# Two-layer cross-attention on one core: where the next batch's layer-0 projections stand among the heads of layer 1

## What is computed

```python
q = hidden_state @ Wq + bq          # layer 0: 32 heads of 16
k = encoder_hidden_state @ Wk + bk  # 8 heads of 16
v = encoder_hidden_state @ Wv + bv
scores = einsum('bkgld,bksd->bkgls', q, k) * scale + mask
out = einsum('bkgls,bksd->bkgld', softmax(scores), v) ... @ Wo + bo
x = layer_norm(out + hidden_state) * gamma + beta

a = layer_norm(audio_kv)            # layer 1, audio_kv is the same context
Q, K, V = hidden_states @ Wq.T, a @ Wk.T, a @ Wv.T    # 16 heads of 32
out = einsum('bhts,bhsd->bhtd', softmax(Q K^T * scale), V) @ Wo.T
return hidden_states + tanh(gate) * out
```

## Time and profile before

| | us |
|---|---|
| median of 3 runs | 1476.19 |
| lowest and highest run | 1471.12, 1485.24 |
| the profiled execution | 1483.69 |
| its span, first to last instruction | 1481.9 |
| mean granted clock of TensorE in it | 0.941 |

### The profile page before, as it was taken

The page is one execution under the profiler, slowest core; times in us unless marked ns, Lnnn a source line. Parts: engine busy times, 40 slices in busy tenths (PEclk is TensorE's granted clock), DMA queues, the critical chain, the costliest instruction groups (busy, mean ns, idle before and its releaser), DMA issues.

```text
span 1481.9 us, 32160 instructions
## 1 busy us (share of the span) xinstructions
PE 1390.0 (94%) x9840; PEld 1008.5 (68%) x9840; DVE 822.4 (55%) x2470; ACT 827.6 (56%) x2504; POOL 183.5 (12%) x200
## 2 busy tenths in 40 slices
PE   3999999999999999999999999999999999999997
PEld 3667676676767667676676766767676776767765
DVE  4435656565564655646465565656646465564643
ACT  3535746476464756646475564646646475564644
POOL 2100111010011101111020111101011110111100
PEclk8559999999999999999999999999999999999996
DMA  8434254534425453344544424453443544434250
GB/s 238 151 94 92 69 122 99 136 82 119 100 70 120 110 134 70 96 111 86 128 108 109 98 71 117 99 136 77 119 100 75 120 110 121 83 81 109 51 133 6
DMA packets 77581, 153.76 MB, mean 104 GB/s; under 512 B 10272, under 2 KB 46944, under 8 KB 76784
## 3 DMA queue, kind: packets, MB, share of 16 engines
q1 hardware_dynamic: 77552, 153.40, 43.9%
HBM read 113.72 MB, written 39.65 MB: 103 GB/s over the span
## 4 chain that ended last, share of the span: by engine, by line
PE 79%; issue 6%; DVE 6%; ACT 4%; DMA 1%; POOL 1%; SPq 1%; ACTq 0%; DVEq 0%; POOLq 0%
PE TP L363 21%; PE PJ L317 12%; PE SCO L354 10%; PE OA L389 5%; PE PJ L553 4%; PE PJ L411 4%; PE PJ L419 4%; PE PJ L330 4%; PE SCO L358 3%; PE OA L394 2%; ACT PR L864 1%; PE PJ L425 1%; DVE SCO L672 1%; ACT PT L877 1%; DMA PT<-wk 1%
## 5 line engine op out<-in xcount | busy, mean ns | idle before, releaser
L864 ACT ACTIVATE PR<-SCO,MN 100x361 f32<-100x361 f32 x768 | 434.1, 566 | 362.1 <-DVE MN L672 337.4
L672 DVE CUSTOM_DVE_ANT_0 SCO<-SCO,MK 100x361 f32<-100x361 f32 x768 | 413.0, 541 | 381.1 <-PE SCO L354 259.2
L363 PE MATMUL TP<-ident,PR 100*121 100x100 f32 x2304 | 438.7, 303 | 34.3 <-ACT PT L877 28.4
L363 PEld LDWEIGHTS TP<-ident,PR 100*121 100x121 f32 x2304 | 342.6, 200 | 143.2 <-issue 89.7
L877 ACT ACTIVATE PT<-TP 121x300 f32<-121x300 f32 x576 | 239.2, 415 | 6.1 <-PE TP L363 6.0
L354 PE MATMUL SCO<-K0S,Q0S 64*100 64x362 f32 x512 | 213.8, 418 | 11.2 <-DMA K0S<-k_scr 10.1
L354 PEld LDWEIGHTS SCO<-K0S,Q0S 64*100 64x100 f32 x512 | 83.9, 164 | 128.0 <-issue 99.7
L864 ACT ACTIVATION_READ_ACCUMULATOR PR<-SCO,MN 100x1 f32 x768 | 151.5, 197 | 0.0
L358 PE MATMUL SCO<-K1S,Q1S 128*100 128x362 f32 x256 | 111.8, 438 | 3.1 <-ACT Q1S L947 1.2
L999 POOL TENSOR_TENSOR TL<-AT,TH 128x363 fp32r<-128x363 f32 x64 | 64.0, 1001 | 393.8 <-ACT TH L922 393.8
L672 DVE DVE_READ_ACCUMULATOR2_ANT MN<- 100x1 f32 x768 | 108.5, 141 | 0.0
(11 more groups left out here) (124 smaller groups left out, 1821.5 us busy)
## 6 DMA issues: line engine op xcount, KB each, us to landing
K1S<-k_scr SPq DMA_DIRECT2D x128, 364.0 KB, 6.4
k_scr<-K1HL SPq DMA_DIRECT2D x64, 364.0 KB, 3.5
Q0S<-q_scr SPq DMA_DIRECT2D x128, 100.0 KB, 4.3
K0S<-k_scr SPq DMA_DIRECT2D x64, 182.0 KB, 5.2
AT<-ctx_cols SPq DMA_DIRECT2D x16, 722.0 KB, 6.3
NAT<-ctx_rows SPq DMA_DIRECT2D x16, 484.0 KB
q_scr<-QHL SPq DMA_DIRECT2D x16, 400.0 KB, 2.5
k_scr<-KHL SPq DMA_DIRECT2D x32, 182.0 KB, 3.0
```

The lines of the kernel that those rows point to most:

```text
L363: last = pe.transpose(TP[0:SP, k % 2, c * T:(c + 1) * T], PR[0:T, k % 3, c * SP:(c + 1) * SP], ident[0:T, 0:T])
L672: dve.tensor_tensor_reduce(out=bank, in0=bank, in1=mask[0:T, :], scale=scale, scalar=3.4e38, op0=ALU.add, op1=ALU.min, accum_out=MN[0:T, k ...
L864: act.activation(PR[0:T, k % 3, 0:S], SCO[0:T, k % 3, 0:S], ACT.Exp, bias=MN[0:T, k:k + 1], scale=-1.0, accum_out=SM[0:T, k:k + 1]).then_i ...
```

## The change

The steps of the three tables are dealt out anew. The queries' 16 steps go over heads 32 to 36 and no longer 32 to 35; the keys' 12 over heads 34 to 38 and no longer 34 to 37; the values' 12 over heads 41 to 46, two each, and no longer 43 to 46, three each. The conversions of the queries and of the keys on ScalarE and VectorE stand one head later, and the two waits of TensorE that belong to the moved steps move with them.

```diff
-        Q0_STEPS = spans({32: 4, 33: 3, 34: 6, 35: 3})
-        K0_STEPS = spans({34: 3, 35: 3, 36: 3, 37: 3})
-        V0_STEPS = spans({43: 3, 44: 3, 45: 3, 46: 3})
+        Q0_STEPS = spans({32: 4, 33: 3, 34: 3, 35: 3, 36: 3})
+        K0_STEPS = spans({34: 2, 35: 2, 36: 2, 37: 3, 38: 3})
+        V0_STEPS = spans({41: 2, 42: 2, 43: 2, 44: 2, 45: 2, 46: 2})
...
                     if more and k in K0_STEPS:
                         if k == 34:
                             pe.wait_ge(ct_l2, 2 * b + 4)
-                        elif k == 36:
+                        elif k == 37:
                             pe.wait_ge(ct_h2, b + 2)
                             pe.wait_ge(ct_l, b + 2)
...
                     if more and k in V0_STEPS:
-                        if k == 43:
+                        if k == 41:
                             pe.wait_ge(q0_l, 4 * b + 8)
...
# VectorE
-                    if more and k == 36:
+                    if more and k == 37:
                         queries0_low(b + 1)
-                    if more and k == 39:
+                    if more and k == 40:
                         keys0_low(b + 1)
...
# ScalarE
-                    if more and k == 36:
+                    if more and k == 37:
                         queries0_high(b + 1)
-                    if more and k == 38:
+                    if more and k == 39:
                         keys0_high(b + 1)
```

## The result

| | us |
|---|---|
| before, median of 4 runs in this comparison (lowest, highest) | 1473.65 (1467.22, 1485.24) |
| after, median of 4 runs (lowest, highest) | 1555.84 (1548.50, 1562.95) |
| ratio | 1.0516, interval 1.0452 to 1.058 |
| profiled execution after, its span, its mean granted clock | 1550.62, 1548.8, 0.898 |

The change makes the kernel 5% slower; the forecast was 1473 us.

A forecast was written before the change was run, and what follows sets the result against it. TensorE, busy 94% of the span, was taken as the bound. Moved steps -2.3, clock -4.6 and K0S wait +2.0 gave -4.9 us profiled; with clock -2.8, -3.1 for the median: 1473 us, range 1458 to 1485.

The forecast's parts named there:

- Front, trough, rest: Heads 32 to 37, heads 38 to 40, and the remainder to the next batch: -0.5, +0.2, +0.15 us per full-clock stretch.
- Moved waits: TensorE's waits for the context's second half (now head 37) and for q0_l (now head 41): no cost.
- SP's queue: Later key conversion makes head 0 wait 0.4 us for K0S in five full-clock stretches: +2.0 us, bounds 0 and 6.
- the slack of 0.8: Time in us, at full clock, between K0S landing (near 759.7) and head 0's score (760.55) before the change.
- Clock: Clock falls in the stretches from head 32 on: ten of 15 instead of 13, -4.6 us profiled, 2.8 for a median run.
- Rival C: K0S load becomes the wait ending last in most batches, falls as today: +4 us, 1480; chance 0.12.
- rival B: Slower: falls in every stretch, and dearer, at heads 41 to 44: +12.3 us profiled, 1488 to 1496; chance 0.11.
- layer-0 stages other than 67.1 us: Sign of being wrong: the later batches' layer-0 stages, which the change does not touch, no longer taking 67.1 us.
- rival D: TensorE's clock falls after sitting idle through, not from low busy share; falls stay, 1475 us; chance 0.05.

The follow-up runs named there:

- e12: Kernel before with the keys alone as in the change (heads 34 to 38, converted one head later); median 1548.10 us, ratio 1.04.
- e3: Changed kernel with the keys and their conversions back as before, queries and values still spread; median 1514.90 us, ratio 1.0249.
- e5: Changed kernel plus five matmuls that nothing reads at the end of turn 47, where TensorE waits for K0S; median 1479.80 us, ratio 0.9999.
- e14: Kernel before with the keys alone as in the change, plus five matmuls that nothing reads at the end of turn 47; median 1574.07 us, ratio 1.0472.
- e6: Changed kernel plus one matmul that nothing reads in each of heads 42 to 46, the wait for K0S kept; median 1566.45 us.
- e4: Kernel before with head 0 also waiting for the second half of the queries (Q0S); median 1708.15 us.
- e10: Changed kernel with head 0's score moved behind the transposes of the context's first quarter and of head 46; median 1855.98 us, ratio 1.2585.
- e11: Changed kernel with head 0's score behind the context's and head 46's transposes, plus nine unread matmuls in heads 39 and 40; median 1943.16 us, ratio 1.3029.
- e1: Changed kernel with the values back as before (three steps in heads 43 to 46), queries and keys still spread; median 1545.29 us.
- e13: Kernel before with half the value steps moved to heads 39 and 40, the rest in heads 43 to 46; median 1574.54 us, ratio 1.0597.
- e9: Kernel before plus ten matmuls that nothing reads in heads 38 to 40 and four around the batch's end and start; median 1468.85 us, ratio 0.9914.
- e7: Changed kernel plus unread matmuls, one in each of heads 42 to 46 and five at the end of turn 47; median 1486.43 us, ratio 1.0024.
- e2: Kernel before with the values alone spread as in the change (two steps in heads 41 to 46); median 1524.08 us, ratio 1.0244.
- e8: Kernel before plus ten matmuls that nothing reads in heads 38 to 40; median 1493.55 us, ratio 1.0021.

## Why the prediction was wrong

**Front, trough, rest.** Forecast -0.5, +0.2 and +0.15; measured -0.33, -0.04 and, without the new wait, -0.01, and so -0.4 instead of -0.15. Small, and on the right side.

**Moved waits.** Nothing, as forecast.

**SP's queue.** The mechanism was right, the term of +2.0 us too small: 7.4, with ten waits and not five, of 0.74 us in the mean and not 0.4. The load's issue came 0.95 us later (forecast 1.1) and the rest of the stretch ended 0.4 us earlier (forecast 0.15), which together is 0.1 more. Most of the difference is in the slack of 0.8: it ran to the landing, and the score starts 0.2 us behind that (the second copy, issued at 1058.45, lands 4.8 us later, the score starts at 1063.51).

**Clock, the step that failed.** Its term of -4.6 us counted the short falls in the stretches and nothing else. There it even erred against the change: five fall, not ten, and the stretches gained 11.2 us instead of 4.9. But it priced a microsecond of idle time at the seam as a microsecond. In this kernel it can be what a fall of 27 us in the next stage starts from: 7.4 us of waits, with seven such falls behind ten of them, brought 80 us. Rival C named the place and priced it at 6 us; rival B had the sign, at the wrong heads (41 to 44) and a sixth of the size. The text on record listed layer-0 stages other than 67.1 us among the signs of being wrong, and that is where it shows.

**What the rows allowed.** The earlier trace rows held a layer-0 stage of 90.65 us at a mean clock of 0.61. I took it as untouched and looked no further. The clock falls there at 26.58, while TensorE waits 10.1 us for K0S ahead of head 0's first score, and it stays at 0.50 for 78.51 us, in the last 70.71 of which TensorE is busy without a break:

```profile
26.60:105.10 78.50, 70.72 (x266) 47.25 (x267) 32.06 (x97) 33.69 (x98) 12.32 (x10) 0.50 0.48 126
```

Such a wait is far longer than the new ones, but it stands at the same place, and a change that adds idle time there should have carried such a fall as a case.

**The rule of rival D** (a fall needs an engine idle through) fares no better than before: ahead of the changed kernel's long falls no idle piece shown is over 0.97 us. The Trainium skill, "TensorE: Matmul & The Clock Gate", section "A second HAM failure mode: psum-queue depth-cycling", bears on this better: frequent short idle pieces between groups of matmuls can bring the clock down too. The traces agree in kind (pieces of 0.46 and 0.88 us ahead of the fall at 1065.76); that section gives no price. By the rule in section Terms of the same page of the Trainium skill, the penalty is the time at the low clock times the share lost, which gives an estimate of 13.7 us for a 27.31 us fall. The stage shows 11.4, and the measurement decides.

**What is shown.** Late keys are enough for the changed kernel's loss: alone they bring the waits, the 27.3 us falls and 4% (e12), and with them taken back waits and such falls are gone (e3). It is the idle time and not the lateness: with K0S loaded as late, matmuls leave no long fall behind the five full-clock stretches of e5 and e14 in which they filled the wait, against 19 behind 28 with the wait open, and the same matmuls ahead of the wait do not help (e6). A later start without any moved work is worse (e4), and with some 1.1 us of idle time ahead of head 0's score and as much behind it a long fall came in 30 of 30 batches (e10, e11).

**What stays open.** First, which waits bring a fall: 9 of the 28 did not, and their lengths overlap with those that did. Nor is the wait the only source: e1 has two falls of 27.3 us and e13 one with no K0S wait over 0.12 us ahead. Second, the falls of 75 to 79 us. They turn up with as little idle time at the seam as e9 has, and two of 25 runs of the kernel before in one call took 1521 us, about one such fall (99.7 - 67.1 = 32.6) above the rest. By the traces and the spread of the runs they are rarer in before, e5 and e7 than in e2, e3, e8 and e13, and in e2, e3, e5 and twice in e14 they begin 13.65 us after a short fall began. What decides them no run told apart, and so the 2.4% of the spread values (e2) and the time of e14 are described here and not explained. Third, why the short falls came back in e5 and e7, and how much of their time is owed to that.

## What to carry to other kernels

Where TensorE is the bound, price idle time by where it stands and not by its length: look in the trace of before for the longest stretch at the low clock, see which work it covers, and give every change that adds a wait ahead of such work a case with that price. It is a case and not a sum: a wait of the same length may bring nothing. When work is moved to fill one hole in TensorE's schedule, see which hole opens where it came from; and where a load must be late, a few matmuls that nothing reads can be cheaper than a wait (e5: 1479.80 against 1555.84). They are no sure cure: the same five in the kernel with the keys alone late gave nothing (e14: 1574.07 against 1548.10).

## What the runs showed of the hardware

- The granted clock stayed at 0.50 for 23.9, 27.3, 75.1, 78.5 and 81.9 us with TensorE 99 to 100% busy (27.31 of 27.31 and 75.09 of 75.09 in the rows shown; 81.48 of 81.92 in e11). The same lengths came again in different kernels. In the first batch of the kernel before it stayed there for 78.51 us, from 26.58 on, the last 70.71 of them busy.
- In the changed kernel no stretch with a short fall had a long one behind it: the short fall delays the end of the stretch enough for K0S to have landed. Short falls do not keep long ones away in general: the four of e1 all stand behind stretches with one. Nor does it pay by itself to be rid of them: e8, e11 and e13 have none, and more long ones than before had.
- The spread of a kernel's runs goes with its long falls, as far as one trace each can tell: 15 us between the runs of e7, which had none, 134 us between those of e8, whose slowest run had five, worth 143 us together by the stages behind them (100.89, 99.68, 77.41, 100.93 and 99.71 us against 67.1).
